# Two small attentions computed in two score passes: maxima first, then keys by queries with the maximum as extra channels

## The chip, the core and the metric

The kernel runs on one core of one Trainium2 chip. A core has five engines that run their own instruction streams and meet at semaphores: TensorE (PE, matrix products; its loading of weights is listed as PEld), VectorE (DVE), ScalarE (ACT), GpSimd (POOL) and SyncE (SP, which here only issues transfers). PE writes its results into PSUM, eight banks of 512 fp32 values on each of 128 partitions; DVE and ACT read them from there. The metric is the device time of one execution in microseconds (us). For the kernel before it is 2440.8 us, the median of three runs from 2438.59 to 2442.29.

## The reference

The reference takes a batch of 8 sequences of 256 tokens of width 128 (`x`) and 8 contexts of 512 tokens of width 96, all fp32, through four layers. The parts that matter, cut short:

```
# layer 0: self attention (256 keys) and cross attention (512 keys), 16 heads of 64, then a gated MLP
# layer 1: one attention of width 128 over the context, layer norms
# layer 2: heads of 8 channels
def _mha(q_in, kv_in, wq, bq, wk, bk, wv, bv, wo, bo):      # 16 heads, HD = 8
    q, k, v = projections, each (b, 16, tokens, 8)
    scores = jnp.einsum('bhqd,bhkd->bhqk', q, k) * HD ** (-0.5)
    p = jax.nn.softmax(scores, axis=-1)
    o = jnp.einsum('bhqk,bhkd->bhqd', p, v)
    return o.transpose(0, 2, 1, 3).reshape(b, -1, WIDTH) @ wo.T + bo
x = x + _mha(h, h, ...)            # 256 keys: "self2"
x = x + _mha(h, context, ...)      # 512 keys: "cross2"
x = x + mlp(h)
# layer 3: 16 heads of 8, queries and keys rotated and brought to unit length, 512 keys: "l3"
```

Each attention gives, for 16 heads, a table of 256 queries by 256 or 512 keys. The softmax takes the largest score of each query away before the exponential.

## The kernel before, in words

The batch is worked through in four pairs of elements (two streams, `_0` and `_1`). In each pair ten attention phases follow one another: self0, cross0, self2, cross2 and l3, each for both streams. A phase is a loop over units; one unit fills one score bank of 512 columns, so self2 has 16 units (a head each) and cross2 has 32 (half of a head's queries each). Beside each phase runs a chain: the serial work of a layer (norms, projections, turned copies), cut in named steps (table STEPS). `planned` and `due` lay the steps evenly over the units of the phase, and `run_rounds` writes the same order into each engine's stream: the attention's work of unit u, then the chain's steps due by u. Engines run in order, so a step waits for what stands before it on its engine. Beside self2_0 runs the long chain mid1 (with keys2), beside self2_1 mid2 and keys2, beside cross2_0 mid2 and keys3, beside cross2_1 mid3 and keys3. keys3 rotates the keys of layer 3 (`krope`, six dependent DVE operations, L1288 to L1293) and takes their inverse lengths.

In self2 and cross2 the queries of one head stand alone in a zeroed tile, `q_mask`, so that a product over 128 channels touches one head only; POOL copies a head's 32 rows there (`mask`, L1718). A unit then goes:

- PE: `scores` (L779) gives queries by keys in one of three banks SC.
- DVE: `nmax`, minus the maximum along the keys (L1532).
- ACT: exponential with `nmax` as bias, into `probs` (L1089).
- PE: `turn_probs`, four transposes of 128x128 into one of two banks PT (L499), since the next product needs keys on the partitions.
- ACT (even units) or DVE (odd units): copy of the turned bank into `probs_t` (L893, L1545).
- PE, for each group of four heads: `heads_out`, the product with the values (L826); a ninth column of ones in the values gives the sums. DVE copies the result out (L1562).

The phase l3 needs no maximum and computes keys by queries at once. The inverse lengths of its keys come from POOL's `pow` in four steps (`k_norm`, L1692), those of its queries from ACT's square root, for which a table of functions is loaded and the exponential's loaded back (L952). On POOL, `settled` makes each operation wait for those before it; the small `rstd` of each norm (L1642) goes through the same queue.

## Time and profile before

| | |
|---|---|
| median of 3 runs | 2440.8 us |
| profiled execution | 2433.14 us, its span 2431.3 us |
| mean granted PE clock | 0.914 of full speed |
| PE busy | 1921.7 us, 79% of the span |
| DVE busy | 1429.7 us, 59% |
| ACT busy | 1312.9 us, 54% |
| POOL busy | 350.5 us, 14% |
| chain that ended last | PE 56%, DVE 20%, ACT 10%, issue 7%, POOL 3% |

No engine is busy all the time: the end is set by a path that changes from engine to engine. The time outside the span, 1.8 us, is the execution's start and end. A busy PE need not be at its peak, and the ends of matmuls are modelled.

### The profile page before, as it was taken

How to read it: one execution, taken by the hardware profiler on the slowest of the kernel's cores; microseconds unless marked ns; L12 is line 12 of the kernel's file. 1: busy time of each engine (PE TensorE's matmuls, PEld its weight loads, DVE VectorE, ACT ScalarE, POOL GpSimd, SP SyncE). 2: the span in 40 equal slices, each digit the busy share in tenths (PEclk: the TensorE clock that was granted, in tenths of full speed). 3: DMA queues.
4: the chain of work that ended last, by engine and by line, in shares of the span. 5: the costliest groups of instructions: out<-in, count | busy, mean ns of one | idle time of the engine just before them, and what ended most of it. 6: DMA issues, size and time to landing. Idle time of an engine off the chain costs nothing.

```text
span 2431.3 us, 41063 instructions
## 1 busy us (share of the span) xinstructions
PE 1921.7 (79%) x13824; PEld 1468.7 (60%) x13824; DVE 1429.7 (59%) x3311; ACT 1312.9 (54%) x3010; POOL 350.5 (14%) x594
## 2 busy tenths in 40 slices
PE   1899886776789997777768988777678898967767
PEld 1777665554577776554557766555456776655544
DVE  2667566764267665676336757567625675657652
ACT  1556454656455554555645555455555555545555
POOL 0000012331100001232200000123320000022321
PEclk7999998989899998888889999888889999988898
DMA  5000000000000000000000000000000000000000
GB/s 125 7 1 1 1 1 1 1 1 1 18 1 1 1 1 1 1 1 1 1 18 1 1 1 1 1 1 1 1 9 9 1 1 1 1 1 1 1 1 6
DMA packets 23857, 13.71 MB, mean 6 GB/s; under 512 B 9202, under 2 KB 23156, under 8 KB 23636
## 3 DMA queue, kind: packets, MB, share of 16 engines
q1 hardware_dynamic: 23636, 10.92, 2.0%
q8 instruction: 120, 1.97, 0.3%
q14 instruction: 101, 0.83, 0.1%
HBM read 9.86 MB, written 1.05 MB: 4 GB/s over the span
## 4 chain that ended last, share of the span: by engine, by line
PE 56%; DVE 20%; ACT 10%; issue 7%; POOL 3%; SPq 1%; DMA 1%; POOLq 0%; ACTq 0%; DVEq 0%
PE heads_out L826 12%; PE turned L499 8%; PE chain_bank L559 4%; DVE nmax L1532 4%; PE scores L429 3%; PE scores L431 3%; PE scores L430 3%; DVE probs_t L1545 3%; PE chain_bank L499 3%; PE scores L779 2%; PE heads_out L499 2%; PE chain_bank L429 2%; PE queries_m L429 2%; ACT probs L1089 2%; DVE xhat L1217 2%
## 5 line engine op out<-in xcount | busy, mean ns | idle before, releaser
L1532 DVE TENSOR_REDUCE nmax<-scores 128x1 f32<-128x512 f32 (+1 forms) x768 | 522.6, 686 | 167.1 <-PE scores L779 90.1
L499 PE MATMUL turned<-ident,probs 128*128 128x128 f32 x3072 | 497.9, 287 | 59.0 <-ACT probs L1089 52.7
L499 PEld LDWEIGHTS turned<-ident,probs 128*128 128x128 f32 x3072 | 385.1, 147 | 148.8 <-ACT probs L1089 91.0
L826 PE MATMUL heads_out<-probs_t,v 128*9 128x256 f32 (+1 forms) x4096 | 377.2, 413 | 8.3 <-issue 5.1
L1089 ACT ACTIVATE probs<-scores,nmax 128x256 f32<-128x256 f32 (+1 forms) x512 | 278.3, 583 | 135.1 <-DVE nmax L1532 134.8
L1091 ACT ACTIVATE probs<-scores,nmax 128x256 f32<-128x256 f32 (+1 forms) x512 | 293.2, 578 | 43.2 <-DVE nmax L1532 42.2
L893 ACT ACTIVATE probs_t<-turned 128x512 f32<-128x512 f32 x384 | 229.7, 598 | 140.4 <-PE turned L499 134.0
L1642 POOL TENSOR_TENSOR rstd<-var_eps,minus_half 128x2 f32<-128x2 f32 x80 | 58.1, 726 | 1553.9 <-DVE var_eps L1211 1449.9
L1545 DVE COPY probs_t<-turned 128x512 f32<-128x512 f32 x384 | 262.0, 682 | 22.0 <-PE turned L499 21.4
L779 PE MATMUL scores<-k_t,q_mask 128*128 128x256 f32 (+1 forms) x512 | 194.7, 428 | 93.7 <-POOL q_mask L1718 74.1
L826 PEld LDWEIGHTS heads_out<-probs_t,v 128*9 128x9 f32 (+1 forms) x4096 | 167.0, 113 | 148.7 <-issue 60.6
L893 ACT ACTIVATE t_hi<-queries_m 128x256 fp32r<-128x256 f32 (+1 forms) x256 | 98.3, 384 | 175.7 <-PE queries_m L431 174.7
L1718 POOL CAST q_mask<-q_t 32x256 fp32r<-32x256 f32 x384 | 155.6, 405 | 192.3 <-DVE q_t L1264 69.9
L779 PEld LDWEIGHTS scores<-k_t,q_mask 128*128 128x128 f32 x512 | 97.4, 211 | 120.9 <-issue 80.9
L1170 DVE TENSOR_TENSOR t_lo<-queries_m,t_hi 128x256 fp32r<-128x256 f32 (+1 forms) x256 | 107.0, 418 | 77.4 <-ACT t_hi L893 75.5
L1557 DVE TENSOR_TENSOR out_t<-heads_out,scale_t 128x256 f32<-128x256 f32 x128 | 54.4, 425 | 157.1 <-ACT scale_t L893 157.1
L1562 DVE COPY out_t<-heads_out 128x256 f32<-128x256 f32 x96 | 40.7, 424 | 178.3 <-PE heads_out L826 178.2
L893 ACT ACTIVATE scale_t<-heads_out 128x256 f32<-128x256 f32 x128 | 49.3, 385 | 171.8 <-PE heads_out L499 171.8
L429 PE MATMUL queries_m<-x_hi,m_hi 128*128 128x256 f32 (+1 forms) x256 | 95.4, 373 | 48.2 <-DVE t_lo L1170 29.2
L429 PE MATMUL scores<-ctx_hi,t_hi 96*128 96x512 f32 x256 | 117.5, 459 | 0.0
L1091 ACT ACTIVATION_READ_ACCUMULATOR probs<-scores,nmax 128x1 f32 x512 | 103.6, 202 | 0.0
L431 PE MATMUL scores<-ctx_lo,t_hi 96*128 96x512 f32 x256 | 103.5, 404 | 0.0
(319 smaller groups left out, 3496.0 us busy)
## 6 DMA issues: line engine op xcount, KB each, us to landing
out_t<-ctx_dram SPq DMA_DIRECT2D x8, 192.0 KB, 3.1
v<-wqt_dram SPq DMA_DIRECT2D x2, 512.0 KB
wo<-wo_dram SPq DMA_DIRECT2D x2, 512.0 KB, 5.5
x<-x_dram SPq DMA_DIRECT2D x8, 128.0 KB, 2.9
y_dram<-x SPq DMA_DIRECT2D x8, 128.0 KB, 1.8
v<-wkt_dram SPq DMA_DIRECT2D x1, 512.0 KB
probs_t<-wv_dram SPq DMA_DIRECT2D x1, 512.0 KB
wff<-wff_dram SPq DMA_DIRECT2D x1, 512.0 KB, 6.9
```

Source lines behind the costliest of these rows:

```text
L429: nc.tensor.matmul(out, a_hi, b_hi, start=True, stop=False)
L431: return nc.tensor.matmul(out, a_hi, b_lo, start=False, stop=True)
L499: return nc.tensor.transpose(out, in_, ident[:, :])
L779: last = nc.tensor.matmul(out, q_mask[:, h % 4, q], k_t[s][:, h // 4, 0:ph.keys], start=True, stop=True)
L826: last = nc.tensor.matmul(O[rows, 0:S], stationary, probs_t[:, h % ph.slots, kb, :], start=(kb == 0), stop=(kb == ph.kb - 1))
L893: return nc.scalar.activation(out, in_, ACT.Copy, scale=scale)
L1089: last = nc.scalar.activation(out, src, ACT.Exp, bias=shift)
L1091: last = nc.scalar.activation(out, src, ACT.Exp, bias=shift, accum_out=sums[:, qb, h:h + 1])
L1170: return nc.vector.tensor_tensor(out, full, f32(high), ALU.subtract)
L1532: nc.vector.tensor_reduce(out, src, AX.X, ALU.max, negate=True).then_inc(sem["attention_max"], 1)
L1545: nc.vector.tensor_copy(turned_place(ph, u), turned_in_bank(ph, 1)).then_inc(sem["attention_copied1"], 1)
L1718: signal(nc.gpsimd.tensor_copy(q_mask[rows, i, :], f32(q_t[ph.s][rows, g, :])), "attention_mask")
```

## The change

Self2 and cross2 become the kind `shifted` (before: `masked`); the others keep their course. Their scores are computed twice.

- The first pass (`scores_for_max`) is the old `scores` into the banks SC. DVE takes minus the maximum from it, and nothing else reads it.
- After four heads, `shift_queries` writes minus the maxima, split in a high and a low part, into channels 24 and 25 of those heads' queries in `q_stack` (the keys have ones there, set by a memset). `turn_shifted` transposes the four heads again (two transposes into an SC bank), ACT copies them into `q_t` (`shifted_turned`), and POOL copies each head into a second masked tile, `shifted_mask`.
- The second pass (`shifted_scores`) gives keys by queries, two blocks of 128 keys by 256 queries in a bank PT, with the maximum already taken away. ACT's exponential (`shifted_exp`) writes straight into `probs_t`. The transposes of the probabilities, the copies out of them and the biased exponentials are gone. `half_outputs` is the product with the values, after every four exponentials.

The second pass runs `lead` steps behind the first, 7 in self2 and 12 in cross2, so these phases take 23 and 44 steps, and the chain's steps are laid over those. In keys3 the rotation of the keys is cut into five steps, and POOL's four `pow` give way to one square root on ACT between two table loads, with a reciprocal on DVE.

```diff
+        self.turned, self.shifted, self.direct = (kind == k for k in ("turned", "shifted", "direct"))
...
+        self.lead = (7, 12)[self.per_head - 1] if self.shifted else 0
+        self.steps = self.units + self.lead
+        self.halves = 9 if name == "self2" else 2 * PROBS_SLOTS
         self.before = {}
 
+        self.uses = []
+        for step in range(self.units):
+            self.uses.append(("max", step))
+            if step % (4 * self.per_head) == 1 and step > 1:
+                self.uses.append(("turn", step // (4 * self.per_head) - 1))
+        self.uses.append(("turn", QUADS - 1))
...
+    def turn_step(self, g):
+
+        return 4 * (g + 1) * self.per_head + 1
+
+    def unit(self, v):
+
+        return v // (4 * self.per_head), v // 4 % self.per_head, v % 4
...
-        "self2": lambda s: Attention("self2", s, 4, S, masked=True),
-        "cross2": lambda s: Attention("cross2", s, 4, T, masked=True),
...
+        "self2": lambda s: Attention("self2", s, "shifted", S),
+        "cross2": lambda s: Attention("cross2", s, "shifted", T),
...
-    "keys3": "kv0 kv1 krope pow0 pow1 pow2 pow3 kunit khigh",
+    "keys3": "kv0 kv1 krope0 krope1 krope2 krope3 krope4 kroot kunit khigh klow",
...
-        PLAN.append(planned(lanes, PHASES[phase, ps].units if phase else 1))
+        PLAN.append(planned(lanes, PHASES[phase, ps].steps if phase else 1))
...
+            def bank_free(readers, n):
+
+                if n >= 0:
+                    name, count = readers[n]
+                    pe.wait_ge(sem[name], count)
+
+            def scores_for_max(ph, u):
+
+                h, part, s = u // ph.per_head, u % ph.per_head, ph.s
+                n = ph.scores_of(("max", u))
+                bank_free(SCORES_READ, n - 3)
+                pe.wait_ge(sem["attention_mask"], ph.at("mask", h + 1))
+                bank = SC[n % 3]
+                for k, qb in enumerate(range(QB) if ph.per_head == 1 else (part,)):
+                    last = nc.tensor.matmul(bank[:, k * S:k * S + ph.keys], q_mask[:, h % 4, qb * P:(qb + 1) * P],
+                                            k_t[s][:, h // 4, 0:ph.keys], start=True, stop=True)
+                last.then_inc(sem["attention_scores"], 1)
...
+            def turn_shifted(ph, g):
+
+                n = ph.scores_of(("turn", g))
+                bank_free(SCORES_READ, n - 3)
+                pe.wait_ge(sem["attention_shift"], ph.at("shift", g + 1))
+                for qb in range(QB):
+                    last = transpose(SC[n % 3][:, qb * P:(qb + 1) * P], q_stack[ph.s][:, qb, 4 * g:4 * g + 4, :])
+                last.then_inc(sem["attention_scores"], 1)
+
...
+
+                g, half, i = ph.unit(v)
+                n = ph.at("turned_banks", v)
+                bank_free(TURNED_READ, n - 2)
+                pe.wait_ge(sem["attention_shifted_mask"], ph.at("shifted_mask", 4 * g + i + 1))
+                for k in range(2):
+                    kb = 2 * half + k
+                    last = nc.tensor.matmul(PT[n % 2][:, k * S:(k + 1) * S], k_t[ph.s][:, g, kb * P:(kb + 1) * P],
+                                            shifted_mask[:, i, :], start=True, stop=True)
+                last.then_inc(sem["attention_shifted"], 1)
+
+            def half_outputs(ph, w):
...
+
+                g, half, _ = ph.unit(4 * w)
+                pe.wait_ge(sem["attention_exp"], ph.at("exp", 4 * w + 4))
+                if half == 0 and ph.at("out_scaled", g) > 0:
+                    pe.wait_ge(sem["attention_out_scaled"], ph.at("out_scaled", g))
+                for k in range(2):
+                    kb = 2 * half + k
+                    for i in range(4):
+                        last = nc.tensor.matmul(O[32 * i:32 * i + E2 + 1, 0:S], v_heads[ph.name][ph.s][:, kb, 4 * g + i, :],
+                                                half_probs[:, (4 * w + i) % ph.halves, k, :], start=(kb == 0),
+                                                stop=(kb == ph.kb - 1))
+                last.then_inc(sem["attention_heads"], 1)
...
+                if ph.shifted:
+                    for u in range(2):
+                        scores_for_max(ph, u)
+                    yield
+                    for step in range(ph.steps):
+                        v = step - ph.lead
+                        if 2 <= step < ph.units:
+                            scores_for_max(ph, step)
+                        for g in range(QUADS):
+                            if step == ph.turn_step(g):
+                                turn_shifted(ph, g)
+                        if v >= 0:
+                            shifted_scores(ph, v)
+                        if v >= 5 and v % 4 == 1:
+                            half_outputs(ph, v // 4 - 1)
+                        yield
+                    half_outputs(ph, ph.units // 4 - 1)
+                    return
...
+                    yield "kroot"
+                    table_for(ACT.Sqrt)
+                    act.wait_ge(sem["keys3_squares"], rank(s, name) + 1)
+                    nc.scalar.activation(k_norm[:, :, :], k_squares[:, :, :], ACT.Sqrt).then_inc(sem["keys3_root"], 1)
+                    table_for(ACT.Exp)
...
+            def shifted_turned(ph, g):
+                n = ph.scores_of(("turn", g))
+                act.wait_ge(sem["attention_scores"], n + 1)
+                copy(q_t[ph.s][:, g, :], SC[n % 3][:, 0:S]).then_inc(sem["attention_turned_shift"], 1)
+
+            def shifted_exp(ph, v):
+                act.wait_ge(sem["attention_shifted"], ph.at("shifted", v + 1))
+                if v >= ph.halves:
+                    act.wait_ge(sem["attention_heads"], ph.at("heads", (v - ph.halves) // 4 + 1))
+                elif v == 0 and ph.at("heads", 0) > 0:
+                    act.wait_ge(sem["attention_heads"], ph.at("heads", 0))
+                bank = PT[ph.at("turned_banks", v) % 2]
+                nc.scalar.activation(half_probs[:, v % ph.halves, :, :], bank[:, :].rearrange("p (k q) -> p k q", k=2),
+                                     ACT.Exp).then_inc(sem["attention_exp"], 1)
...
-                    yield "krope"
+                    yield "krope0"
                     for r in range(2):
                         key = name, s, f"kv{r}"
                         dve.wait_ge(sem[bank_read(key)], FILL[key])
-                    rotate(heads4(nat_k[s][:, :, :]), TB, k_squares[:, :, :])
+                    for n, _ in enumerate(rotate(heads4(nat_k[s][:, :, :]), TB, k_squares[:, :, :])):
+                        yield f"krope{n + 1}"
                     nc.vector.tensor_scalar(k_squares[:, :, :], k_squares[:, :, :], EPS_L2 ** 2, None, ALU.max
                                             ).then_inc(sem["keys3_squares"], 1)
                     yield "kunit"
-                    dve.wait_ge(sem["keys3_pow"], TB * rank(s, name) + TB)
+                    dve.wait_ge(sem["keys3_root"], rank(s, name) + 1)
+                    then(nc.vector.reciprocal(k_norm[:, :, :], k_norm[:, :, :]))
                     unit_length(heads4(nat_k[s][:, :, :]), TB, k_norm[:, :, :]).then_inc(sem["keys3_keys"], 1)
-                    yield "khigh"
+                    yield "klow"
                     keys_low(name, s, TB)
...
+            def shift_queries(ph, g):
+
+                dve.wait_ge(sem["attention_max"], ph.at("max", 4 * (g + 1) * ph.per_head))
+                high, low = (q_stack[ph.s][:, :, 4 * g:4 * g + 4, c] for c in (24, 25))
+                shift = nmax[:, 4 * g * QB:4 * (g + 1) * QB].rearrange("p (h b) -> p b h", b=QB)
+                then(nc.vector.tensor_copy(f32r(high), shift))
+                nc.vector.tensor_tensor(f32r(low), shift, high, ALU.subtract).then_inc(sem["attention_shift"], 1)
...
+                if ph.shifted:
+                    for u in range(2):
+                        maximum(ph, u)
+                    yield
+                    for step in range(ph.steps):
+                        if 2 <= step < ph.units:
+                            maximum(ph, step)
+                        if step < ph.units and (step + 1) % (4 * ph.per_head) == 0:
+                            shift_queries(ph, step // (4 * ph.per_head))
+                        v = step - ph.lead - 2
+                        if v > 0 and v % (4 * ph.per_head) == 0:
+                            quad_copy(ph, v // (4 * ph.per_head) - 1)
+                        yield
+                    quad_copy(ph, QUADS - 1)
+                    return
...
-                    for kb in range(TB):
-                        yield f"pow{kb}"
-                        settled()
-                        pool.wait_ge(sem["keys3_squares"], rank(s, name) + 1)
-                        signal(nc.gpsimd.tensor_tensor(k_norm[:, kb, :], k_squares[:, kb, :], minus_half[:, :], ALU.pow),
-                               "keys3_pow")
...
+                    yield "t0"
+                    settled()
+                    pool.wait_ge(sem["attention_turned_shift"], PHASES["self2", s].at("turned_shift", QUADS))
+                    signal(nc.gpsimd.memset(q_stack[s][:, :, :, 24:32], 0.0), "pads")
...
+            def mask_shifted(ph, h):
+
+                g, i = h // 4, h % 4
+                if i == 0:
+                    pool.wait_ge(sem["attention_turned_shift"], ph.at("turned_shift", g + 1))
+                used = ph.at("shifted", 4 * g * ph.per_head - 3 + i if g else 0)
+                if used:
+                    pool.wait_ge(sem["attention_shifted"], used)
+                settled()
+                rows = slice(32 * i, 32 * i + 32)
+                signal(nc.gpsimd.tensor_copy(shifted_mask[rows, i, :], f32(q_t[ph.s][rows, g, :])),
+                       "attention_shifted_mask")
+
...
+                for step in range(ph.steps):
+                    if 0 < step < ph.units and not ph.turned:
+                        h, part = divmod(step + 3, ph.per_head)
+                        if part == 0 and h < H:
+                            mask(ph, h)
+                    for h in range(H * ph.shifted):
+                        if step == max(ph.lead + 4 * (h // 4 * ph.per_head - 1) + h % 4, ph.turn_step(h // 4)):
+                            mask_shifted(ph, h)
                     yield
 
```

The order of the instructions moves with it. PE in the middle of cross2_0, before (`queries_m` and `chain_bank` are banks of the chain, `scores` are SC, `turned` are PT):

```order
L779 MATMUL scores<-k_t,q_mask 128x512
L499 MATMUL turned<-ident,probs 128x128 x4
L779 MATMUL scores<-k_t,q_mask 128x512
L499 MATMUL turned<-ident,probs 128x128 x4
L779 MATMUL scores<-k_t,q_mask 128x512
L499 MATMUL turned<-ident,probs 128x128 x4
L779 MATMUL scores<-k_t,q_mask 128x512
L499 MATMUL turned<-ident,probs 128x128 x4
L779 MATMUL scores<-k_t,q_mask 128x512
L499 MATMUL turned<-ident,probs 128x128 x4
L499 MATMUL queries_m<-ident,v 128x128 x4
```

The same place in the changed kernel:

```order
L827 MATMUL scores<-k_t,q_mask 128x512
L848 MATMUL turned<-shifted_mask,k_t 128x256 x2
L545 MATMUL chain_bank<-ident,xhat 128x128 x2
L827 MATMUL scores<-k_t,q_mask 128x512
L848 MATMUL turned<-shifted_mask,k_t 128x256 x2
L827 MATMUL scores<-k_t,q_mask 128x512
L848 MATMUL turned<-shifted_mask,k_t 128x256 x2
L827 MATMUL scores<-k_t,q_mask 128x512
L545 MATMUL scores<-ident,out_t 128x128 x2
L848 MATMUL turned<-shifted_mask,k_t 128x256 x2
L861 MATMUL heads_out<-probs_t,v 9x256 x8
L827 MATMUL scores<-k_t,q_mask 128x512
```

Where each score product was followed by four transposes, it is now followed by two products of 256 columns, with two transposes of queries into `scores` once in eight steps. PE near the start of cross2_0, from the chain's turning of `heads_nat`, before:

```order
L779 MATMUL scores<-k_t,q_mask 128x512
L499 MATMUL turned<-ident,probs 128x128 x4
L499 MATMUL chain_bank<-ident,heads_nat 128x128 x2
L779 MATMUL scores<-k_t,q_mask 128x512
L499 MATMUL turned<-ident,probs 128x128 x4
L779 MATMUL scores<-k_t,q_mask 128x512
L499 MATMUL turned<-ident,probs 128x128 x4
L559 MATMUL chain_bank<-wo_sa,out_t 128x128 x2
L779 MATMUL scores<-k_t,q_mask 128x512
```

And in the changed kernel:

```order
L827 MATMUL scores<-k_t,q_mask 128x512 x2
L545 MATMUL chain_bank<-ident,heads_nat 128x128 x2
L827 MATMUL scores<-k_t,q_mask 128x512 x3
L545 MATMUL scores<-ident,out_t 128x128 x2
L605 MATMUL chain_bank<-wo_sa,out_t 128x128 x2
L827 MATMUL scores<-k_t,q_mask 128x512 x3
L848 MATMUL turned<-shifted_mask,k_t 128x256 x2
```

Until its first products into `turned`, only the first pass stands between the chain's products, for 12 steps. POOL from the start of cross2_0, before (`v` holds the keys' stack, `k_norm` the inverse lengths):

```order
L1718 CAST q_mask<-q_t 32x256
L1654 CAST v<-v 128x32x8
L1718 CAST q_mask<-q_t 32x256 x7
L1642 TENSOR_TENSOR rstd<-var_eps,minus_half 128x2
L1692 TENSOR_TENSOR k_norm<-k_squares,minus_half 128x16
L1718 CAST q_mask<-q_t 32x256 x2
L1692 TENSOR_TENSOR k_norm<-k_squares,minus_half 128x16
L1718 CAST q_mask<-q_t 32x256 x2
L1692 TENSOR_TENSOR k_norm<-k_squares,minus_half 128x16
```

And in the changed kernel:

```order
L1880 CAST q_mask<-q_t 32x256 x5
L1892 CAST shifted_mask<-q_t 32x256 x3
L1880 CAST q_mask<-q_t 32x256
L1892 CAST shifted_mask<-q_t 32x256
L1880 CAST q_mask<-q_t 32x256
L1805 TENSOR_TENSOR rstd<-var_eps,minus_half 128x2
L1880 CAST q_mask<-q_t 32x256 x2
L1892 CAST shifted_mask<-q_t 32x256 x3
L1880 CAST q_mask<-q_t 32x256
L1892 CAST shifted_mask<-q_t 32x256
```

The four `pow` are gone, and three copies into `shifted_mask` stand in a row among the others. On ACT the two table loads of the new square root stand in a row between two exponentials of the second pass, and POOL's copies into `q_mask` now wait for each other as well.

## Rows read from the trace of the kernel before

**Rows 1.** Busy time by engine (count), PEclk in the third pair's four phases, and DMA.
```profile
1527.60:1593.60 66.00, 47.85 (x300) 37.84 (x298) 38.52 (x94) 29.11 (x67) 12.05 (x26) 0.82 0.00 1
1593.60:1629.40 35.80, 27.86 (x219) 20.64 (x219) 23.39 (x49) 22.17 (x52) 7.72 (x20) 0.90 0.01 2
1629.40:1687.30 57.90, 44.41 (x331) 32.41 (x332) 42.36 (x82) 33.74 (x59) 20.30 (x25) 0.91 0.00 1
1687.30:1759.20 71.90, 50.78 (x373) 34.91 (x372) 47.28 (x96) 41.52 (x73) 21.07 (x25) 0.89 0.00 1
```

**Rows 2.** Chain that ended last, shares by line, in these four stretches, in order.
```profile
by line: PE heads_out L826 8.7%; PE chain_bank L559 8.5%; PE turned L499 8.5%; DVE xhat L1217 5.7%; issue 5.4%; PE chain_bank L499 4.9%; PE chain_bank L649 4.3%; POOL rstd L1642 4.2%; PE scores L779 4.1%; PE queries_m L649 3.9%; DVE probs_t
...
by line: PE heads_out L826 13.5%; PE turned L499 13.4%; PE scores L779 13.1%; PE queries_m L499 10.3%; issue 9.6%; ACT probs L1089 4.4%; PE chain_bank L499 4.1%; DVE probs_t L1545 3.8%; ACT k_t L893 3.4%; PE chain_bank L429 2.6%; ACT v L893
...
by line: PE turned L499 13.5%; issue 12.2%; PE scores L779 9.7%; DVE nmax L1532 8.2%; PE heads_out L826 8.1%; ACT probs L1089 7.2%; POOL k_norm L1692 5.0%; PE queries_m L499 4.2%; DVE probs_t L1545 3.5%; POOL q_mask L1718 2.1%; ACT v L893 1
...
by line: issue 11.3%; DVE nmax L1532 9.4%; PE heads_out L826 8.4%; ACT probs L1089 6.4%; PE turned L499 6.1%; ACT L952 6.0%; DVE probs_t L1545 5.9%; PE scores L779 5.0%; POOL k_norm L1692 4.0%; PE chain_bank L740 2.9%; PE chain_bank L559 2.
```

**Rows 3.** Pieces of that chain, PE: start us, us, what; low clock, then high.
```profile
1562.59 0.43 PE scores L779 x2
1563.02 0.85 PE turned L499 x4
...
1602.09 0.24 PE scores L779 x2
1602.33 0.44 PE turned L499 x4
...
1664.21 1.84 PE heads_out L826 x32
```

**Rows 4.** Groups by line and form: busy us, mean ns; idle before.
```profile
L1532 DVE TENSOR_REDUCE nmax<-scores 128x1 f32<-128x512 f32 x512 | 347.6, 686 | 129.4 <-PE scores L779 69.5 <-PE scores L431 56.2
L1545 DVE COPY probs_t<-turned 128x512 f32<-128x512 f32 x384 | 262.0, 682 | 22.0 <-PE turned L499 21.4
L893 ACT ACTIVATE probs_t<-turned 128x512 f32<-128x512 f32 x384 | 229.7, 598 | 140.4 <-PE turned L499 134.0
...
L1089 ACT ACTIVATE probs<-scores,nmax 128x512 f32<-128x512 f32 x256 | 172.6, 688 | 88.3 <-DVE nmax L1532 88.0
L1718 POOL CAST q_mask<-q_t 32x256 fp32r<-32x256 f32 x384 | 155.6, 405 | 192.3 <-DVE q_t L1264 69.9 <-PE scores L779 43.9 <-PE scores L796 32.0
...
L893 ACT ACTIVATE scale_t<-heads_out 128x256 f32<-128x256 f32 x128 | 49.3, 385 | 171.8 <-PE heads_out L499 171.8
...
L1550 DVE RECIPROCAL inv<-sums 128x4 f32<-128x4 f32 x128 | 21.5, 168 | 0.0
```

**Rows 5.** Timeline: POOL's pow, and PE's longest waits for a mask.
```profile
1653.30 2.90 POOL L1692 TENSOR_TENSOR k_norm<-k_squares,minus_half 128x16 f32<-128x16 f32 x1
...
1656.89 0.76 PE L779 MATMUL scores<-k_t,q_mask 128*128 128x512 f32 x1 [4.07 <-POOL q_mask L1718]
...
1730.39 0.77 PE L779 MATMUL scores<-k_t,q_mask 128*128 128x512 f32 x1 [4.96 <-POOL q_mask L1718]
```

**Rows 6.** Chain that ended last, cross2_0: first and last piece of krope.
```profile
1643.55 0.33 DVE rope_tmp L1288
...
1647.15 0.20 DVE k_squares L1451
```

**Rows 7.** Timeline, ACT in cross2_1 around the queries' square root.
```profile
1745.49 0.69 ACT L1089 ACTIVATE probs<-scores,nmax 128x512 f32<-128x512 f32 x1 [2.46 <-DVE nmax L1532]
1746.20 1.28 ACT L952 ACT_TABLE_LOAD   x1
...
1747.60 0.21 ACT L1063 ACTIVATE q_norm<-q_squares 128x32 f32<-128x32 f32 x1
1747.83 1.28 ACT L952 ACT_TABLE_LOAD   x1
...
1749.24 0.67 ACT L1089 ACTIVATE probs<-scores,nmax 128x512 f32<-128x512 f32 x1
```

191 lines of the change are left out of this document (107 added, 84 removed).

## The prediction, made before the changed kernel had run

> **What bounds the kernel now.** I read three views: the busy times of stretches, the chain of waits for the same stretches, and the single rows of what stands on that chain. In the third of the four pairs, the phases that the change touches take 66.0, 35.8, 57.9 and 71.9 us, 231.6 us together [rows 1], so about 926 of the 2433 us. In none of them is an engine full. The chain of waits shows who counts [rows 2]: in self2_0 the serial steps of mid1 (`chain_bank`, `xhat`, `rstd`), with the attention's PE work in between; in the others the attention's own PE work, then DVE's maxima and copies and ACT's exponentials. Nothing else in the program changes by more than a few waits. So the question is what each edit takes off this mixed path and what it puts there. I count per pair and multiply by four.
>
> **What goes.**
>
> The transposes. They hold 8.5, 13.4, 13.5 and 6.1% of the path [rows 2], that is 5.6 + 4.8 + 7.8 + 4.4 = 22.6 us. Four of them take 0.44 us at the high clock and 0.85 at the low one; two products of 256 columns take 0.24 and 0.43 [rows 3]. So the second pass costs half: -11.3 us. All of the pair's 96 units would give more: with the mean granted clocks of 0.82 to 0.91 [rows 1], about a fifth of the time is at the low level: 0.20 x 0.8 + 0.42 x 0.2 = 0.24 us a unit, 23 us. But of the transposes' time, 96 x (0.44 x 0.8 + 0.85 x 0.2) = 50 us, only 45% is on the path, so I stay with 11.3.
>
> The copies out of the turned banks. DVE's are on the path for 3.8, 3.5 and 5.9% of the last three phases [rows 2]: 1.4 + 2.0 + 4.2 = -7.6 us. In self2_0 the share is cut off, but under 3.9%, at most 2.6 us more. ACT's copies of 0.60 us [rows 4] I leave at nothing, since ACT is busy for only half of these phases; they are a reserve.
>
> The exponentials. The unbiased one of 512 columns isn't in the trace in this form: it lies between 0.60 (ACT's copy of the same size) and 0.69 (the biased one) [rows 4]; I take 0.60, because the new exponential, like the copy, has no bias. On the path they have 7.2 and 6.4% in cross2, 8.8 us, of which 13% go: -1.1.
>
> POOL's `pow`. Each takes 2.90 us, and a mask behind it makes PE wait 4.07 and 4.96 us, once in each cross2 [rows 5]. These waits go: -9.0 us. What is late next there is a `q_mask` behind a copy of 0.41 us instead of 2.90.
>
> The rotation of the keys. In cross2_0 it holds DVE, and the path, from 1643.55 to 1647.35 [rows 6], 3.8 us; I take the same for cross2_1. Cut in five, each piece stands beside a unit in which DVE has lost its copy. I count half of it as hidden: -3.8 us (0 to -7.6).
>
> Together -32.8 us a pair.
>
> **What comes.**
>
> Opening and closing. The second pass starts 7 or 12 steps late. In these steps DVE needs 0.69 for a maximum [rows 4] where PE needs 0.24, and at the end ACT needs 0.60 where PE needs 0.24 and the product with the values, which is as before. If nothing filled these gaps of 0.45 and at most 0.36, they would cost 7 x 0.81 = 5.7 in each self2 and 12 x 0.81 = 9.7 in each cross2, 31 us a pair. But the chain's steps are laid over them too and need PE's free time, self2_0 is paced by mid1 in any case, and DVE's maxima were on the path before (8.2 and 9.4% in cross2). I take 5 us, between 0 and 31, near the low end for these three reasons.
>
> The shift. For each of 16 quads in a pair: two small DVE operations of at least 0.17 each (the nearest is a reciprocal of 4 elements, 168 ns), ACT's copy of 256 columns, 0.385 [rows 4], and two transposes, half of 0.44 [rows 3]. That is 5.4 us on DVE, 6.2 on ACT, 3.5 on PE. A third to a half of DVE's and PE's will be exposed: +3 (0 to 9).
>
> The square root. From the end of the exponential before to the start of the next, the queries' root takes 1746.18 to 1749.24, 3.06 us [rows 7]. Two in a pair hold ACT for 6.1 us, with PE two banks ahead at most; I count half: +3 (0 to 6.1). The reciprocal is in it. The Trainium skill (ScalarE: Activation LUTs, What ACT_TABLE_LOAD costs) says a switch to another set costs about 2.66 us, a load of 1283 ns and a drain behind it; by that the two switches would take 5.3 us and this term would be up to 10.6. The trace agrees with the load and not with the drain: the work behind a load starts 0.1 to 0.3 us after it.
>
> POOL's queue. 64 more masks a pair of 0.405 us [rows 4] are 26 us on an engine that is busy for 61 of 232 us; they displace 23 us of `pow`. But an `rstd` can now stand behind three masks, 1.2 us, and eight `rstd` a pair are on a chain's path: +2 (0 to 10). The extra memsets go with this.
>
> Together +13 us, so -19.8 a pair and -79 us in all. Against the profiled execution of 2433.1 us that is 2354; the median of the runs stands 7.7 us higher, which I add: **2362 us**.
>
> **The rivals.**
>
> 1. The gain is larger. PE, DVE and ACT all lose work in every unit, and waits between them shrink too ("issue" is 12.2% of cross2_0 [rows 2]). All that goes at its upper end is 11.3 + 10.2 + 1.1 + 9.0 + 7.6 = 39.2, with 4 coming back: -35 a pair, 2301. Against it: self2_0 is a serial chain.
>
> 2. Opening and closing eat more: 15 instead of 5, as DVE and ACT alone set the pace for 24 of 44 steps. -10 a pair, 2401. For it speaks that cross2's attention alone has about the same bound by its slowest engine: 12 x 0.69 + 20 x 0.48 + 12 x 0.60 = 25.1 against 32 x 0.68 = 21.8, both without the values' product.
>
> 3. The clock. The stretch with the most idle PE has the lowest granted clock, 0.82, against 0.91 in cross2_0 [rows 1], and the rows at the low level cost about twice [rows 3]. With PE emptier at both ends of every phase, all four could run at 1.2 GHz: per unit 0.86 us instead of 0.57, 96 x 0.29 x 45% = 12 us, and the chain's products some 4 more. -4 a pair, 2425. The Trainium skill (TensorE: Matmul & The Clock Gate, What's actually happening) states that the throttled clock is the default and activity releases it, which speaks for this rival.
>
> 4. Slower: the round to shift a quad. From the last maximum of a quad to its first shifted product the work is 0.69 + 0.34 (DVE), 0.22 to 0.43 (PE), up to 0.60 waiting for an exponential and 0.385 (ACT), 0.41 and two semaphores (POOL): about 2.9 us. In self2 four steps lie between, in cross2 five; at 0.71 us a step (0.24 + 0.24 and the values' product, 1.84 for eight units [rows 3]) self2's slack is 2.8 us, just used up. A masked copy, an `rstd` or a table load in between makes PE wait at every quad. From 19.8 / 16 = 1.24 us a quad on the change loses; at 2 us it is +12 a pair, 2489. Against it: the steps have lasted 1.8 us or more (57.9 / 32).
>
> That the change doesn't do what it says is hardly open: the order shows the four transposes gone.
>
> **How the numbers follow.** Forecast 0.42, rival 1 0.21, rival 2 0.17, rival 3 0.09, rival 4 0.11. A measurement here can tell about 0.2%, 5 us, from no change. Faster by more: 0.42 + 0.21 + 0.16 + 0.05 = 0.84; within it 0.05; slower 0.11, with the far end of the costs (31 + 9 + 6 + 10 against half the gains: +40 a pair) inside rival 4. The range goes from rival 1's 2301, less a little, to rival 3's 2425: 2295 to 2430.
>
> **What would show it.** Right: `turned` is filled by pairs of 256-column products, DVE busy falls by about 4 x (48 x 0.68 - 5) = 110 us and ACT's by 100 to 140 us, the waits for `q_mask` of 4 to 5 us are gone, cross2_0 and cross2_1 are each 6 to 10 us shorter, self2_0 about 3, and the phases outside keep their times within 1 us. Rival 2: in the first 12 steps of cross2 a step takes 0.9 us or more with PE waiting for `nmax`. Rival 3: the granted clock of these phases at 0.75 or less. Rival 4: PE waits over 1 us for `shifted_mask` at most quads. Wrong altogether: a longer self2_0, which would mean that the chain's steps wait on POOL.

## The result, and the profile after

The changed kernel takes 2318.5 us (median of 4 runs, 2315.3 to 2326.5) against 2441.6 (2438.6 to 2445.2) for the kernel before on the same chip: a ratio of 0.9498 [0.9477, 0.9518], 5.0% or 123 us less. The forecast was 2362, 79 us less; the result lies 44 us below it, inside the range, and nearer to rival 1 (2301). The profiled execution has a span of 2313.5 us (before 2431.3) and a mean granted clock of 0.92 (0.914).

The windows of the four phases of the third pair, columns as in [rows 1], are these:

```profile
1476.30:1538.90 62.60, 44.54 (x282) 35.42 (x282) 34.56 (x95) 22.55 (x47) 18.34 (x44) 0.84 0.00 1
1538.90:1569.80 30.90, 22.99 (x196) 16.86 (x192) 20.22 (x49) 15.12 (x32) 14.26 (x36) 1.00 0.01 1
1569.80:1615.50 45.70, 36.54 (x290) 23.98 (x282) 34.25 (x75) 26.48 (x52) 16.10 (x36) 1.00 0.01 1
1615.50:1675.80 60.30, 47.57 (x337) 31.77 (x338) 39.47 (x90) 35.58 (x68) 16.52 (x39) 0.89 0.00 1
```

They answer to [rows 1]: -3.4, -4.9 and -12.2 us in the first three. The fourth window of [rows 1] ends at the first product of l3 and leaves out 36 matmuls, while this one ends at l3's first exponential. Up to the same event the kernel before has

```profile
1687.70:1761.90 74.20, 53.08 (x409) 36.35 (x409) 47.67 (x97) 41.59 (x74) 22.15 (x27) 0.89 0.00 1
```

so cross2_1 is 13.9 us shorter, and the pair about 34. The granted clock went from 0.90 and 0.91 to 1.00 in self2_1 and cross2_0. Busy time in the whole span fell from 1429.7 to 1335.2 us on DVE (-94.5), from 1312.9 to 1205.2 on ACT (-107.7) and from 1921.7 to 1852.8 on PE.

The groups by line and form (busy us, mean ns; idle before), where [rows 4] stood:

```profile
L1678 DVE TENSOR_REDUCE nmax<-scores 128x1 f32<-128x512 f32 x512 | 344.0, 685 | 96.2 <-PE scores L477 59.2 <-PE scores L827 32.6
...
L1220 ACT ACTIVATE probs_t<-turned 128x512 f32<-128x512 f32 x384 | 219.9, 597 | 121.1 <-PE turned L848 114.9
...
L848 PE MATMUL turned<-shifted_mask,k_t 128*128 128x256 f32 x768 | 177.2, 321 | 26.7 <-ACT probs_t L1220 22.1 <-POOL shifted_mask L1892 3.8
...
L1892 POOL CAST shifted_mask<-q_t 32x256 fp32r<-32x256 f32 x256 | 102.0, 398 | 221.5 <-ACT q_t L1005 158.7 <-PE turned L848 22.9 <-POOL shifted_mask L1892 22.3
...
L1699 DVE COPY probs_t<-turned 128x512 f32<-128x512 f32 x192 | 130.7, 681 | 9.6 <-PE turned L545 9.5
...
L545 PE MATMUL scores<-ident,out_t 128*128 128x128 f32 x128 | 28.4, 308 | 23.7 <-DVE out_t L1686 23.7
...
L1686 DVE TENSOR_TENSOR out_t<-nmax,out_t 128x8 fp32r<-128x8 f32 x64 | 12.6, 197 | 2.2
```

The exponential without a bias lasts 597 ns, as taken. Half of DVE's copies out of the turned banks are gone (192 stand of 384; those left belong to self0 and cross0). PE idled 22.1 us in all for exponentials ahead of the shifted products, 23.7 us for DVE's part of the shift ahead of the two transposes of `turn_shifted`, and only 3.8 us, over 64 quads, for `shifted_mask`.

The chain of waits by line, cross2_0 and then cross2_1:

```profile
by line: DVE nmax L1678 20.5%; PE turned L848 14.8%; PE heads_out L861 12.9%; issue 8.9%; ACT probs_t L1220 6.4%; PE scores L827 5.3%; ACT L1064 4.0%; PE queries_m L545 3.2%; PE scores L545 2.3%; PE chain_bank L545 2.1%; DVE nat_k L1586 1.9
by line: PE heads_out L861 13.0%; DVE nmax L1678 12.2%; PE turned L848 9.3%; PE scores L827 6.5%; issue 5.8%; ACT probs_t L1220 5.7%; ACT L1064 4.3%; PE chain_bank L786 3.4%; PE chain_bank L605 3.3%; PE queries_m L786 2.9%; ACT v L1005 2.3%
```

Against [rows 2] DVE's maxima went from 8.2 to 20.5% of the shorter cross2_0. PE's longest waits there, in the timeline, that bear on the change:

```profile
1588.13 0.41 PE L545 MATMUL scores<-ident,out_t 128*128 128x128 f32 x2 [1.44 <-DVE out_t L1686]
1604.53 0.99 PE L848 MATMUL turned<-shifted_mask,k_t 128*128 128x256 f32 x4 [1.33 <-ACT probs_t L1220]
1662.18 0.66 PE L545 MATMUL scores<-ident,out_t 128*128 128x128 f32 x2 [2.14 <-DVE out_t L1686]
```

The waits of 4.07 and 4.96 us of [rows 5] have no successor in these four phases. What is late is a shift of a quad, or an exponential behind a table load.

### The profile page after: what moved, and what is told of

It reads as the page before. It is cut to its first block, busy times and chain, and to the rows that moved or that the text cites. A ratio compares the mean times of both kernels' runs of the same rounds, so it can differ in the third digit from the quotient of the medians.

```text
span 2313.5 us, 40668 instructions
## 1 busy us (share of the span) xinstructions
PE 1852.8 (80%) x13184; PEld 1406.7 (61%) x13184; DVE 1335.2 (58%) x3255; ACT 1205.2 (52%) x2794; POOL 365.3 (16%) x835
## 4 chain that ended last, share of the span: by engine, by line
PE 59%; DVE 22%; ACT 9%; issue 5%; DMA 2%; POOL 1%; SPq 1%; POOLq 0%; ACTq 0%; DVEq 0%
PE heads_out L922 9%; DVE nmax L1678 6%; PE turned L545 5%; PE chain_bank L605 4%; PE heads_out L861 3%; PE scores L475 3%; PE scores L477 3%; PE scores L476 3%; PE chain_bank L545 3%; PE turned L848 3%; PE heads_out L545 2%; PE scores L827 2%; PE chain_bank L475 2%; PE queries_m L475 2%; ACT L1064 2%
## 5 line engine op out<-in xcount | busy, mean ns | idle before, releaser
L1204 ACT ACTIVATE probs<-scores,nmax 128x256 f32<-128x256 f32 (+1 forms) x512 | 292.9, 577 | 43.1 <-DVE nmax L1678 42.3
L1220 ACT ACTIVATE probs_t<-turned 128x512 f32<-128x512 f32 x384 | 219.9, 597 | 121.1 <-PE turned L848 114.9
L922 PE MATMUL heads_out<-probs_t,v 128*64 128x256 f32 (+1 forms) x2560 | 266.1, 402 | 3.2 <-ACT probs_t L1230 3.2
L545 PE MATMUL turned<-ident,probs 128*128 128x128 f32 x1536 | 239.5, 279 | 5.1 <-ACT probs L1204 4.6
L545 PEld LDWEIGHTS turned<-ident,probs 128*128 128x128 f32 x1536 | 192.9, 145 | 46.2 <-ACT probs L1204 11.1
L848 PE MATMUL turned<-shifted_mask,k_t 128*128 128x256 f32 x768 | 177.2, 321 | 26.7 <-ACT probs_t L1220 22.1
L827 PE MATMUL scores<-k_t,q_mask 128*128 128x256 f32 (+1 forms) x512 | 173.5, 396 | 24.8 <-DVE nmax L1678 12.2
L922 PEld LDWEIGHTS heads_out<-probs_t,v 128*64 128x64 f32 (+1 forms) x2560 | 127.6, 121 | 92.0 <-issue 25.0
L848 PEld LDWEIGHTS turned<-shifted_mask,k_t 128*128 128x128 f32 x768 | 134.3, 206 | 67.1 <-ACT probs_t L1220 51.4
L1005 ACT ACTIVATE probs_t<-turned 128x512 f32<-128x512 f32 x192 | 114.9, 598 | 64.7 <-PE turned L545 59.7
L1892 POOL CAST shifted_mask<-q_t 32x256 fp32r<-32x256 f32 x256 | 102.0, 398 | 221.5 <-ACT q_t L1005 158.7
L1699 DVE COPY probs_t<-turned 128x512 f32<-128x512 f32 x192 | 130.7, 681 | 9.6 <-PE turned L545 9.5
L475 PE MATMUL queries_m<-x_hi,m_hi 128*128 128x256 f32 (+1 forms) x256 | 96.5, 377 | 48.5 <-DVE t_lo L1308 29.3
L827 PEld LDWEIGHTS scores<-k_t,q_mask 128*128 128x128 f32 x512 | 90.4, 201 | 52.8 <-DVE nmax L1678 28.9
```

The costliest lines, as they stand in the source:

```text
L475: nc.tensor.matmul(out, a_hi, b_hi, start=True, stop=False)
L545: return nc.tensor.transpose(out, in_, ident[:, :])
L827: last = nc.tensor.matmul(bank[:, k * S:k * S + ph.keys], q_mask[:, h % 4, qb * P:(qb + 1) * P], k_t[s][:, h // 4, 0:ph.keys], start=True, ...
L848: last = nc.tensor.matmul(PT[n % 2][:, k * S:(k + 1) * S], k_t[ph.s][:, g, kb * P:(kb + 1) * P], shifted_mask[:, i, :], start=True, stop=True)
L922: last = nc.tensor.matmul(O[rows, 0:S], stationary, probs_t[:, h % ph.slots, kb, :], start=(kb == 0), stop=(kb == ph.kb - 1))
L1005: return nc.scalar.activation(out, in_, ACT.Copy, scale=scale)
```

## The experiments

"Cost" is the difference of a kernel's ratio from 0.9498, in us of 2441.6; each ratio has an interval of about ±0.25%, so a difference under some 8 us is not told from nothing. The phases, in us, are means over the four pairs of the profiled execution, from first maximum to first maximum (cross2_1: to l3's first exponential). Four times the sum of the phases' changes is up to 20 us off the cost, because the profiled execution is one of several and phases that an edit doesn't touch move too. Self2_0 is such a phase: in the run without root, which changes nothing there, it takes 62.7, 62.6, 65.5 and 66.0 us in the four pairs, with the granted clock at 0.84, 0.84, 0.82 and 0.79.

| kernel | ratio, interval | cost | self2_0 | self2_1 | cross2_0 | cross2_1 |
|---|---|---|---|---|---|---|
| before | 1 | +123 | 66.3 | 35.1 | 57.6 | 74.5 |
| after | 0.9498 [0.9477, 0.9518] | 0 | 62.7 | 30.9 | 45.7 | 60.3 |
| before, new keys3 | 0.9933 [0.9907, 0.9960] | +106 | 67.1 | 35.1 | 58.8 | 70.2 |
| cross2 one pass | 0.9850 [0.9823, 0.9876] | +86 | 62.8 | 30.9 | 57.7 | 72.3 |
| self2 one pass | 0.9600 [0.9578, 0.9623] | +25 | 65.9 | 35.5 | 46.9 | 60.9 |
| `pow` back | 0.9739 [0.9715, 0.9764] | +59 | 62.7 | 30.9 | 55.6 | 67.2 |
| rotation whole | 0.9694 [0.9668, 0.9719] | +48 | 65.3 | 30.9 | 50.7 | 66.0 |
| no root, no tables | 0.9469 [0.9436, 0.9501] | -7 | 64.2 | 30.9 | 45.3 | 60.3 |
| lead 10 | 0.9667 [0.9639, 0.9696] | +41 | 62.8 | 30.9 | 52.8 | 63.7 |
| lead 16 | 0.9631 [0.9605, 0.9658] | +33 | 64.0 | 30.9 | 52.7 | 61.8 |
| products twice | 0.9665 [0.9640, 0.9690] | +41 | 65.3 | 32.1 | 47.8 | 62.5 |
| maxima twice | 1.0500 [1.0480, 1.0521] | +245 | 74.3 | 40.8 | 68.4 | 78.5 |
| lead 10, products twice | 0.9821 [0.9788, 0.9853] | +79 | 65.0 | 32.1 | 51.3 | 68.1 |
| maximum of half the keys | 0.9342 [0.9324, 0.9360] | -38 | 61.9 | 31.5 | 43.0 | 58.4 |

**Only the new keys3, in the kernel before.**

```diff
-    "keys3": "kv0 kv1 krope pow0 pow1 pow2 pow3 kunit khigh",
+    "keys3": "kv0 kv1 krope0 krope1 krope2 krope3 krope4 kroot kunit khigh klow",
```

> The kernel before with the edits to keys3 alone: the rotation of the keys in five steps and the square root on ACT in place of POOL's pow; both small attentions stay as before. Theory A (the terms of the prediction add up): 9.0 + 3.8 us a pair go and 3 come, -39 us, 2402. Theory B (a wait of PE costs more than its length, because the clock is low after it): -55 us or more, 2387 or less, with a granted clock above 0.95 in cross2_0. Theory C (ACT's two table loads stand in the way of biased exponentials that everything waits for): no gain, 2430 to 2445.

Measured 2433.1 us: 0.7% faster, about 16 us. That is in C's range of times, though not no gain; A's 39 us and B's 55 didn't come. The timeline shows what took the place of the wait for a mask in cross2_0, PE first and then ACT:

```profile
1686.33 1.11 PE L500 MATMUL turned<-ident,probs 128*128 128x128 f32 x4 [3.27 <-ACT probs L1095]
```
```profile
1682.54 1.28 ACT L953 ACT_TABLE_LOAD   x1
...
1683.94 0.24 ACT L1029 ACTIVATE k_norm<-k_squares 128x64 f32<-128x64 f32 x1
1684.20 1.28 ACT L953 ACT_TABLE_LOAD   x1
...
1685.60 1.25 ACT L1095 ACTIVATE probs<-scores,nmax 128x512 f32<-128x512 f32 x2
```

In one pass PE's transposes wait for each biased exponential, so the root's 3.06 us on ACT (1682.54 to 1685.60) come through to PE as a wait of 3.27: the wait of 4.07 is exchanged. In cross2_1 the wait of 4.96 gives way to three waits for `q_mask` of 2.77, 2.16 and 2.48 us. The masks stand behind a norm's `rstd` in POOL's queue:

```profile
1719.43 0.70 POOL L1655 TENSOR_TENSOR rstd<-var_eps,minus_half 128x2 f32<-128x2 f32 x1 [14.39 <-DVE var_eps L1217]
1720.24 1.75 POOL L1725 CAST q_mask<-q_t 32x256 fp32r<-32x256 f32 x4
```

So `pow` was not the only thing that made masks late.

**One pass kept in one pair of phases.** Twice the kernel after, with the old way (biased exponential, four transposes, copies) for cross2, then for self2:

```diff
-        "cross2": lambda s: Attention("cross2", s, "shifted", T),
+        "cross2": lambda s: Attention("cross2", s, "masked", T),
```

> The changed kernel with cross2 in one pass as before, self2 in two, and the new keys3. The two cross2 phases gained 26 us a pair together. Theory A: 10 of it is keys3, so that 16 come back, +64 us, 2383. Theory B (keys3's part is larger, since the waits for masks were followed by a low clock): +40 us or less, 2359. Theory C (keys3 is worth little, the two passes all): +95 us or more, 2413.

> The changed kernel with self2 in one pass as before and cross2 in two. Theory A (each phase's gain is its own): the two self2 phases are 3.3 and 4.4 us longer again, +31 us, about 2350. Theory B (self2's gain came from the clock and the neighbours): under +12 us, below 2331.

Measured 2413.1 and 2351.6 us. The two passes in cross2 are worth 86 us in the presence of the rest, nearer to C's 95 than to A's 64; those in self2 25, nearer to A's 31. Cross2 in one pass, windows of its two phases:

```profile
1618.00:1675.70 57.70, 44.08 (x332) 31.45 (x330) 42.95 (x82) 36.91 (x64) 8.90 (x21) 0.91 0.00 1
1675.70:1748.00 72.30, 54.47 (x409) 38.33 (x408) 48.06 (x97) 45.13 (x78) 10.48 (x24) 0.88 0.00 1
```

DVE has 8.7 and 8.6 us more to do than after, ACT 10.4 and 9.6, PE 7.5 and 6.9; each phase is 12.0 us longer. That is more than any one engine's added work. PE's share of it is 7.5 us of work and 4.5 of idle time in cross2_0, 6.9 and 5.1 in cross2_1; the granted clock of cross2_0 is 0.91 instead of 1.00, so part of that work is the lower clock.

**`pow` back, in the kernel after.**

```diff
-                    nc.scalar.activation(k_norm[:, :, :], k_squares[:, :, :], ACT.Sqrt).then_inc(sem["keys3_root"], 1)
...
+                        signal(nc.gpsimd.tensor_tensor(k_norm[:, kb, :], k_squares[:, kb, :], minus_half[:, :], ALU.pow),
```

> The changed kernel with POOL's four pow back in keys3 and no square root on ACT; the rotation stays in five steps. Theory A (the terms of the prediction): 9.0 us a pair of waits come back and 3 us of table loads go, +24 us, 2342. Theory B (twice as many masks stand behind pow now, and the clock falls in each wait): +45 us or more, 2363. Theory C (with the second pass 12 steps late, masks are made early enough and the waits stay hidden): within 8 us of 2318, or faster by the table loads.

Measured 2384.5 us, B. The granted clock of cross2_0 is 0.88 to 0.91 instead of 1.00. POOL's timeline, and PE's:

```profile
1645.30 2.90 POOL L1850 TENSOR_TENSOR k_norm<-k_squares,minus_half 128x16 f32<-128x16 f32 x1 [0.43 <-POOL shifted_mask L1892]
...
1649.18 2.90 POOL L1850 TENSOR_TENSOR k_norm<-k_squares,minus_half 128x16 f32<-128x16 f32 x1 [0.34 <-POOL out_t L1805]
1652.23 0.82 POOL L1892 CAST shifted_mask<-q_t 32x256 fp32r<-32x256 f32 x1 [0.16 <-POOL k_norm L1850]
```
```profile
1653.20 0.47 PE L848 MATMUL turned<-shifted_mask,k_t 128*128 128x256 f32 x2 [3.58 <-POOL shifted_mask L1892]
```

POOL has the shifted masks as well now, and they stand behind each `pow`. In the kernel before this edit and the cut rotation together were worth 16 us; here this edit alone is worth 59.

**Rotation in one step.**

```diff
-                    for n, _ in enumerate(rotate(heads4(nat_k[s][:, :, :]), TB, k_squares[:, :, :])):
-                        yield f"krope{n + 1}"
+                    for _ in rotate(heads4(nat_k[s][:, :, :]), TB, k_squares[:, :, :]):
+                        pass
```

> The changed kernel with the rotation of layer 3's keys in one step again, the square root on ACT kept. Theory A (the prediction's term: half of 3.8 us is hidden by cutting): 3.8 us a pair come back, +15 us against the changed kernel. Theory B (in two passes DVE has room, and PE has two or three banks to work on while DVE rotates): within 6 us. Theory C (the burst holds the maxima, and the clock falls behind it, as behind the pow waits): +30 us or more.

Measured 2370.8 us, C. DVE's timeline and PE's wait behind it:

```profile
1601.56 0.41 DVE L1426 TENSOR_TENSOR rope_tmp<-nat_k,rope_sin 128x256 f32<-128x256 f32 x1
...
1604.67 0.69 DVE L1435 TENSOR_REDUCE k_squares<-rope_tmp 128x64 f32<-128x512 f32 x1
...
1605.50 1.28 DVE L1678 TENSOR_REDUCE nmax<-scores 128x1 f32<-128x512 f32 x2
```
```profile
1606.24 0.79 PE L827 MATMUL scores<-k_t,q_mask 128*128 128x512 f32 x1 [3.04 <-DVE nmax L1678]
```

3.9 us on DVE without a maximum make PE wait 3.04, and cross2_0 is 5.0 us longer, cross2_1 5.7, more than the block lasts. (Self2_0's 2.6 us more stand in a phase that this edit doesn't touch.)

**No square root and no table loads** (the root is left out, a copy stands for it).

```diff
-                    table_for(ACT.Sqrt)
-                    nc.scalar.activation(k_norm[:, :, :], k_squares[:, :, :], ACT.Sqrt).then_inc(sem["keys3_root"], 1)
-                    table_for(ACT.Exp)
+                    copy(k_norm[:, :, :], k_squares[:, :, :]).then_inc(sem["keys3_root"], 1)
```

> The changed kernel with a copy in place of the keys' square root and without its two table loads; it leaves out the square root, so the keys of layer 3 have another length. Theory A (the prediction's term, half exposed): 3 us a pair go, -12 us against the changed kernel. Theory B (PE's waits for ACT's exponentials in the trace, 1.33 and 1.31 us, are all that it costs): -5 to -10 us. Theory C (ACT has so much room that nothing changes): within 4 us.

Measured 2312.4 us, 7 us under after, with overlapping intervals; cross2_0 is 0.4 us shorter and cross2_1 the same. So PE's waits of 1.33 and 1.31 us behind ACT in the trace after bring back 0.4 us together. That PE has other steps to do while ACT loads is the likely reason.

**Another lead.** The second pass of cross2 10, then 16 steps behind the first.

```diff
-        self.lead = (7, 12)[self.per_head - 1] if self.shifted else 0
+        self.lead = (7, 10)[self.per_head - 1] if self.shifted else 0
```

> The changed kernel with cross2's second pass 10 steps behind the first instead of 12 (42 steps instead of 44). In the trace of the changed kernel cross2_0 takes 13.4 us until its first exponential and 11.5 us after its last maximum, of 45.7. Theory A (the opening is paced by DVE and the chain, the closing by ACT): each step less saves 0.4 to 0.8 us in each of the eight phases, -6 to -13 us. Theory B (the round of the shift becomes late: 2 steps less for turning, copying and masking a quad): PE waits at the four quads of a phase, +15 us or more. Theory C (the steps are paced by the chain, which is the same): within 4 us.

> The changed kernel with cross2's second pass 16 steps behind the first instead of 12 (48 steps). Theory A of the run before: +13 to +26 us. Theory B (the round was just in time at 12, so 16 hides more): -5 us or less. Theory C: within 4 us.

Measured 2363.5 and 2356.5 us: both lose. Lead 10 has B's sign: over the whole kernel PE's waits for `shifted_mask` rise from 3.8 to 19.4 us, and those for `nmax` ahead of first-pass products from 12.2 to 22.0.

```profile
PE scores L827 <- DVE nmax L1678: 22.0, 32, 1.1
PE turned L848 <- POOL shifted_mask L1892: 19.4, 20, 2.9
```

Lead 16 costs more (33 us) than A's 13 to 26, and B and C fail; the same PE work lasts 41.2 us in three of its four cross2_0 instead of 36.6, at a granted clock of 0.93. Windows of cross2_0, after with lead 12 and then with lead 10:

```profile
1569.80:1583.20 13.40, 9.04 (x62) 6.11 (x54) 10.39 (x24) 1.76 (x5) 3.78 (x10) 1.00 0.00 1
1583.20:1603.90 20.70, 17.74 (x145) 11.91 (x143) 19.47 (x43) 15.24 (x30) 8.45 (x19) 1.00 0.00 1
1603.90:1615.50 11.60, 9.76 (x86) 5.97 (x86) 4.38 (x10) 9.48 (x20) 3.87 (x8) 1.00 0.01 2
```
```profile
1594.60:1604.00 9.40, 6.84 (x49) 4.47 (x49) 6.53 (x15) 1.15 (x3) 2.38 (x7) 1.00 0.00 1
1604.00:1626.00 22.00, 18.60 (x121) 12.74 (x119) 18.16 (x40) 11.38 (x21) 7.69 (x17) 0.84 0.00 1
1626.00:1647.60 21.60, 16.64 (x125) 10.16 (x124) 10.20 (x22) 14.96 (x28) 5.80 (x13) 0.92 0.01 2
```

The same work keeps PE busy for 36.5 us with lead 12 and for 42.1 with lead 10. The granted clock, 1.00 throughout with lead 12, falls with lead 10 after the ninth us, although no wait of PE in that phase is longer than 1.2 us (1.5 with lead 12). Whether it is cause or consequence the next run asks.

**First-pass products twice,** with lead 12 and with lead 10 (the second product of each is redundant; the products of l3 are issued twice too, in a part of the edit not shown here):

```diff
-                    last = nc.tensor.matmul(bank[:, k * S:k * S + ph.keys], q_mask[:, h % 4, qb * P:(qb + 1) * P],
-                                            k_t[s][:, h // 4, 0:ph.keys], start=True, stop=True)
+                    for _ in range(2):
+                        last = nc.tensor.matmul(bank[:, k * S:k * S + ph.keys], q_mask[:, h % 4, qb * P:(qb + 1) * P],
+                                                k_t[s][:, h // 4, 0:ph.keys], start=True, stop=True)
```

> The kernel after, with every score product of the first pass (also in the phases that kept one pass per head pair in the last stage) issued twice into the same bank. The second is redundant; the output is unchanged. Theory A (PE's work on the path costs what it lasts): in a pair 96 units get a second product pair of 0.24 us at the high clock, 45% of it on the path, so +10 us a pair, some +41 us in all, 2360. Theory B (the extra PE work keeps the granted clock up where it is 0.84 to 0.89, self2_0, cross2_1 and the last stage, and PE has idle time there anyway): those phases keep or lower their times, so that the whole is within 12 us of after. Clock by phase tells them apart: B wants 0.93 or more in self2_0 and cross2_1.

> The second pass of cross2 10 steps behind instead of 12, as in the run with a lead of 10, and the first-pass products issued twice. Theory A (lead 10 loses because the granted clock falls to 0.90 in cross2_0 when PE has more idle time): the extra products bring the clock back to about 1.00 and cross2_0 to 46 to 49 us instead of 52.8, so the whole is at or under the 2363 of lead 10. Theory B (lead 10 loses by waits, and the clock follows): the extra PE work comes on top, cross2_0 at 53 or more and the whole at 2375 to 2405.

Measured 2360.2 and 2400.6 us. With lead 12 the price is A's 41 us, in part by luck: the four phases that A counted got 8.1 us a pair longer, 32 in all, and the rest is mostly l3, which A didn't count. In cross2_0 6.3 us more of PE's work made the phase 2.1 longer. The clock in cross2_1 did rise, 0.89 to between 0.89 and 0.97, but the phase got 2.2 us longer all the same. Windows of cross2_0, lead 12 and lead 10:

```profile
1593.10:1640.90 47.80, 42.86 (x324) 29.50 (x322) 34.68 (x75) 27.32 (x52) 16.07 (x36) 1.00 0.01 2
```
```profile
1608.80:1660.10 51.30, 44.00 (x323) 29.75 (x322) 34.72 (x74) 27.79 (x52) 15.69 (x36) 1.00 0.01 2
```

This splits lead 10's loss in cross2_0. With more PE work the clock stays at 1.00 there, and the phase is 1.5 us shorter than with lead 10 alone, although PE has 32 more pairs of products to do: so the clock is a cause of its own. But at the same clock lead 10 is still 3.5 us longer than lead 12. Taken as a difference of differences, about half of the 7.1 us are waits (3.5) and half the clock (3.6). That supposes that the doubled products hide as much waiting with either lead, which no run shows; by the two windows above, 5.5 us are the same work lasting longer and the rest idle time. Neither theory had the size: A's 46 to 49 us didn't come, and the whole was B's.

**DVE's maxima twice.**

```diff
+                if ph.shifted:
+                    then(nc.vector.tensor_reduce(out, src, AX.X, ALU.max, negate=True))
```

> The kernel after, with DVE's maximum of each unit in the two-pass phases taken twice (384 more of 0.69 us, same output). Theory A (opening of a phase is paced by DVE's maxima, as the steps of 1.21 us before the first exponential suggest): in each phase the opening gets 7 or 12 times up to 0.69 longer and the rest some, 24 to 40 us a pair, +100 to +160 us. Theory B (DVE, busy for 58%, has free time; the maxima are on 12 to 20% of the path): 96 x 0.69 x about 0.17 = 11 us a pair, +45. Theory C: DVE hides it all, under +15.

Measured 2568.6 us, +245: 384 more maxima of 0.69 us cost 0.64 each, above A's upper end and slower than the kernel before. In cross2_0 the opening (12 steps) went from 13.4 to 20.8 us, 0.62 a step, and the middle (20 steps) from 20.7 to 34.7, 0.70 a step: not the opening alone. Window of cross2_0, and its chain by line:

```profile
1717.80:1787.20 69.40, 48.41 (x291) 31.07 (x290) 55.87 (x107) 27.09 (x52) 16.11 (x37) 0.75 0.00 1
```
```profile
by line: DVE nmax L1679 28.4%; DVE nmax L1680 25.2%; issue 8.1%; PE heads_out L861 6.7%; PE turned L848 5.6%; PE scores L545 1.9%; PE chain_bank L545 1.7%; ACT probs_t L1220 1.7%; DVE out_t L1718 1.4%; DVE nat_k L1586 1.2%; ACT v L1005 1.1%
```

DVE is 81% busy here, against 75% after, and the granted clock fell from 1.00 to 0.75: PE's same work lasts 48.4 us instead of 36.5. So the 0.64 us per maximum hold the clock's part as well as DVE's.

**Maximum over half of the keys** (the other half's is left out; the quotient stays the same while the exponentials are in range).

```diff
+                if ph.shifted:
+                    src = src[:, :, 0:P] if ph.per_head == 1 else src[:, 0:S]
                 nc.vector.tensor_reduce(out, src, AX.X, ALU.max, negate=True).then_inc(sem["attention_max"], 1)
```

> The kernel after, with the maximum of each unit in the two-pass phases taken over half of the keys; the maxima of the other half are left out (the quotient of the softmax does not depend on the number subtracted, as long as the exponentials stay in range, so the output can stay the same). The reduction of 256 columns should last about 0.35 to 0.43 instead of 0.69, so 384 times about 0.3 us less on DVE, 115 us in all. Theory A (DVE's maxima pace the whole of each phase, as 384 more of them cost 250 us, 0.65 each): 0.94 of it comes back, 100 us or more, 2220 or less. Theory B (they pace only the openings: 7 + 7 + 12 + 12 steps a pair): 38 x 4 x 0.3 = 45 us, 2274. Theory C (the share of the chain of waits: 9, 19, 20 and 12% of the four phases, 28 us a pair for 96 maxima): 0.43 of it goes, 12 us a pair, 2270, but with the gain spread over opening and middle. Theory D (nothing, since PE is right behind): 2305 or more.

Measured 2289.2 us, between C and D, 6.6% under before:

```profile
L1680 DVE TENSOR_REDUCE nmax<-scores 128x1 f32<-128x256 f32 x256 | 102.7, 419 | 51.8 <-PE scores L827 48.5
```
```profile
1552.20:1594.50 42.30, 36.27 (x292) 24.19 (x290) 26.10 (x74) 25.95 (x51) 16.81 (x37) 1.00 0.01 2
```

Each maximum is 0.27 us shorter, 103 us in all, and 38 came back, 0.37 of it (by the phases of the profiled execution only 19; self2_1 got 0.6 us longer, at a clock of 0.95 in three of its four instances). In cross2_0 the opening is 1.9 and the middle 1.8 us shorter. DVE's time costs nearly its full length when added and a third or less when removed. The likely reading is that the kernel after stands at a bend, where PE (86% busy here) takes over. This version isn't a general one, since a key outside the half could be far above its maximum.

## Why the prediction was right, and where its sizes were off

Direction and place were as forecast, and the time lies in the range. But 2318.5 is some 17 us from rival 1's 2301, which had a chance of 0.21, and 44 from the forecast. The net was -30.8 us a pair instead of -19.8. One order of the runs splits it: the new keys3 in the kernel before brought -4.1 a pair, where the sum had -9.0 - 3.8 + 3 = -9.8; the two passes on top of it brought -26.6 (106 us), where the sum had -10. One part was taken at more than twice its size and the other at well under half, so that the total came this near is partly luck. By its own steps:

**The waits for `pow` and the root (-9.0 and +3).** The forecast put PE's waits of 4.07 and 4.96 us down to `pow`, and the reading of what would be late next ("a `q_mask` behind a copy of 0.41 us") was wrong for cross2_1. What PE waited for `q_mask` ahead of these scores, in us over the whole kernel (times, longest), in the kernel before, with the new keys3 alone, with cross2 in one pass, and after:

```profile
PE scores L779 <- POOL q_mask L1718: 74.1, 32, 5.0
PE scores L780 <- POOL q_mask L1725: 66.2, 36, 4.3
PE scores L880 <- POOL q_mask L1890: 48.2, 28, 2.8
PE scores L827 <- POOL q_mask L1880: 4.6, 4, 1.2
```

The new keys3 alone took 7.9 us of these waits and not 36; the two passes took the other 61.6, 15.4 a pair, 43.6 of them in cross2. The sum held nothing for that. Not all of it is gain: in self2_0 a wait of 4.3 us for a mask went, and those for `xhat` rose from 4.3 to 9.2. Why the masks are in time in two passes no run isolates. Taken out of the kernel after, the edit for `pow` is worth 14.7 a pair (59 us). The table loads' +3 was too high: without root and loads the kernel gains 1.7 a pair, not told from nothing. What neither end of the sum held is that the two passes and this edit need each other: in one pass the loads reach PE, in two the `pow` would sit in front of twice the masks.

**The rotation (-3.8, 0 to -7.6).** Undone, it costs 12.0 us a pair, above the upper end, since the bound was what DVE held on the path. Run whole in the new kernel, it starves the first pass and the granted clock goes with it (cross2_0 at 0.93 instead of 1.00). Part of that cost is a fault of the new order, not a gain over before: in the kernel before, this and `pow` together brought only 4.1.

**Transposes, copies, exponentials (-11.3, -7.6, -1.1).** Together with opening, closing, shift and POOL's queue they were to bring -10 a pair in all (-20 and +10). The two experiments with one pass kept give -21.5 for cross2 (86 us) and -6.2 for self2 (25 us). For self2 half of the transposes' 10.4 us and the copies' 1.4, with a third of the 10 coming back, make -3.3, against the -6.2 measured. For cross2 6.1 + 6.2 + 1.1, with two thirds coming back, make -6.7, against -21.5: mis-sized by a factor of three.

The step that failed is the weighting: work was priced by its share of the chain of waits (DVE's copies 1.4 + 2.0 + 4.2 of 33 us; 45% of PE's transposes), and waits that weren't named were left at nothing. Cut at the same events, the four phases of the third pair went from 234.3 to 199.6 us, of which PE was busy for 173.6 and 151.7 and idle for 60.7 and 47.9. PE's work fell by 21.9 us, clock included, about the 23 that the forecast worked out for all 96 units and set aside for 11.3; its idle time fell by 12.8. That is an account, not a proof that all of it was on the path. The run with doubled maxima shows what added DVE work costs in these loops, 0.93 of its length with the clock's part in it, and the one with halved maxima 0.37 or less; doubled products cost a third in cross2_0. The copies removed, 48 x 0.68 = 33 us a pair, may lie on the dear side. How the 26.6 divide among copies, transposes, masks and clock stays open, since no run put only one of them back.

**The clock, not in the sum.** Rival 3 had it fall; it rose to 1.00 in self2_1 and cross2_0. What it is worth: cross2_0 with the same work keeps PE busy for 42.1 us at a granted clock of 0.90 and 36.5 at 1.00, and the pair of runs with doubled products puts its part in the length at about 3.6 us. The Trainium skill (TensorE: Matmul & The Clock Gate, What's actually happening) has activity release the clock; PE's busy share agrees for cross2_0 (77% before, 80% after) but falls in self2_1 (78% to 74%), whose clock rose as well. So the share over a phase doesn't tell it, and what does stays open.

**Opening and closing (+5).** The opening of cross2_0 runs at 13.4 / 12 = 1.12 us a step, over the 0.9 set for rival 2, with DVE 78% busy, though PE waits only 1.4 us for `nmax` in the whole phase. So half of what rival 2 was to show is there, but not its 2401 us: the middle runs at 20.7 / 20 = 1.04 us a step, against 57.9 / 32 = 1.81 over the phase before. The bound that spoke for rival 2 was misread. It took PE's 0.68 a unit for the slowest engine before, but DVE had 0.69 for the maximum and half of 0.68 for the copy, 1.03, so 33.0 us and not 21.8; with 0.69 in the middle as well, the new bound is 29.3 and not 25.1. By its slowest engine cross2 gets shorter. The cost of opening and closing alone wasn't isolated; a shorter lead (10) didn't lower the phase.

**Shift (+3, 0 to 9) and rival 4.** The mask of the shift made PE idle for 3.8 us in 64 quads, 0.06 each against the 1.24 at which rival 4 decides. PE's waits behind DVE's part of the shift are larger, 23.7 us, 5.9 a pair: three in each cross2, the longest 1.44 and 2.14, and one of 0.28 in self2_1. So the +3 was low, inside its bounds.

**What was forecast by row.** DVE busy -94.5 (110 said), ACT -107.7 (100 to 140), self2_0 -3.6 (3; but this phase moves by 3 us with the clock alone), cross2_0 and cross2_1 -11.9 and -14.2 (6 to 10 said, too small). Phases outside weren't all within 1 us: l3_1 went from 44.2 to 46.5, cross0_1 from 97.3 to 99.4, self0_0 from 44.0 to 45.2, some 5 us a pair given back. Their work is unchanged; their clock isn't (l3_1 0.83 to 0.87 before, 0.78 to 0.81 after). So rival 1 was right on the phases, -34 a pair, and what was lost outside brought the result back to -30.8.

**Not additive.** Undone one at a time, two passes in cross2, in self2, `pow` and rotation cost 86 + 25 + 59 + 48 = 218 us; all together brought 123. The two attentions do add: 86 + 25 = 111, against 106 for both on top of the new keys3. What doesn't add is keys3 with the two passes: undone in the kernel after, its two edits cost 59 and 48, while in the kernel before they brought 16 together. Two passes with the whole old keys3 were not run.

## What to carry to other kernels

Where DVE, PE and ACT are each 60 to 80% busy and hand work round, a share of the chain of waits is only the first-order price: add up each engine's work per unit as well, double the suspected work and halve it, and read both slopes. A wait put down to one slow operation in a queue can stay when that operation goes: look at what else stands in the queue. Edits made together for one purpose should be priced in the kernel that has the others, since one edit may bring back a wait that another has hidden. After moving work, compare the granted clock of every phase, also of those that weren't touched, before putting a difference down to a wait.

## What the runs showed of the hardware

An untouched phase, cross0_1, lasts 96.7 us at a granted clock of 0.96 and 101.6 at 0.90, with PE busy for 82.9 and 88.7 us (the first pair, before and after). Two steps of lead moved a stretch of 46 us from 1.00 to 0.90, and redundant products brought it back to 1.00.

The table load took 1.28 us every time. A one-column operation that the kernel puts behind each load started 0.01 us after it, and the next exponential 0.12 us after it (the load from 1684.20 to 1685.48, the exponential at 1685.60, in the run with the new keys3 alone). A DVE maximum over 512 columns lasts 0.685 us, over 256 0.419.
